# Turning a pair's first block of gathered rows one step earlier in an expert loop on Trainium2

## What is computed

```python
cap = int(math.ceil(CAP_FACTOR * K * N / E))          # 2 * 16384 / 8 = 4096 rows for each expert
disp = jnp.zeros((E, cap, D), x.dtype).at[e_flat, p_flat].add(x_rep * kmask[:, None])
h = jax.nn.gelu(jnp.einsum('ecd,edh->ech', disp, w1) + b1[:, None, :], approximate=False)
y = jnp.einsum('ech,ehd->ecd', h, w2) + b2[:, None, :]
yk = y[e_flat, p_flat]
w = gvals.reshape(-1).astype(x.dtype)
out = (yk * w[:, None]).reshape(N, K, D).sum(axis=1)
```

## Time and profile before

| | us |
|---|---|
| median of 3 runs | 5787.27 |
| lowest and highest | 5783.33, 5816.49 |
| the profiled execution's own time | 5797.3 |
| its span, from the first instruction to the last | 5795.6 |
| TensorE busy in it | 5178.6 (89%) |
| VectorE busy | 2885.5 (50%) |
| mean granted TensorE clock | 0.924 |

### The profile page before, as it was taken

One profiled execution on the slowest core, in us unless ns is written; L12 is line 12 of the kernel. 1 busy time (PEld: TensorE's weight loads), 2 busy tenths in 40 slices (PEclk: granted clock), 3 DMA queues, 4 the chain that ended last, 5 costly groups with the idle time before them and its releaser, 6 DMA issues. The chain is left out here.

```text
span 5795.6 us, 218499 instructions
## 1 busy us (share of the span) xinstructions
PE 5178.6 (89%) x98967; PEld 3339.4 (58%) x98967; DVE 2885.5 (50%) x6705; ACT 1707.7 (29%) x2823; POOL 941.6 (16%) x940
## 2 busy tenths in 40 slices
PE   5999999999999999999999857899999999999990
PEld 3556565665656556566565644566665666666660
DVE  6667676777767667676776639211111111111116
ACT  3433333343333334333333310111121121112113
POOL 0000000000000000000000000344444445445440
PEclk9899998999999999999999868999999999999995
DMA  1000000000000000000000000222222222222227
GB/s 31 22 19 26 26 23 29 19 29 23 22 30 19 29 23 22 30 19 29 23 22 29 15 31 4 62 32 49 53 32 49 38 47 49 38 47 34 38 31 236
DMA packets 211402, 207.31 MB, mean 36 GB/s; under 512 B 57314, under 2 KB 199715, under 8 KB 210467
## 3 DMA queue, kind: packets, MB, share of 16 engines
q0 software_dynamic: 57984, 69.29, 7.6%
q1 hardware_dynamic: 135970, 108.67, 6.1%
q10 hardware_dynamic: 16640, 16.78, 0.9%
HBM read 107.08 MB, written 85.49 MB: 33 GB/s over the span
## 5 line engine op out<-in xcount | busy, mean ns | idle before, releaser
L1473 PE MATMUL bank<-gathered_T,w1s 128*128 128x512 f32 x2048 | 951.5, 625 | 88.1 <-DVE gathered_T L1411 88.1
L1484 PE MATMUL bank<-w2s,hidden_T 128*128 128x256 f32 x4096 | 894.6, 379 | 0.0
L1484 PEld LDWEIGHTS bank<-w2s,hidden_T 128*128 128x128 f32 x4096 | 775.8, 190 | 117.7 <-issue 15.3
L1443 ACT ACTIVATE hidden_T<-bank,b_expert 128x512 f32<-128x512 f32 x512 | 351.8, 687 | 1588.7 <-PE bank L1473 1588.7
L1473 PEld LDWEIGHTS bank<-gathered_T,w1s 128*128 128x128 f32 x2048 | 408.5, 201 | 593.4 <-issue 591.8
L1418 DVE TENSOR_TENSOR result_rows<-bank,b2s 128x512 f32<-128x512 f32 x128 | 88.6, 692 | 1169.3 <-PE bank L1484 1169.3
L1150 POOL MEMSET tri<- 128x128 f32 x1 | 0.2, 210 | 3436.3 <-POOLq L337 3436.3
L1369 POOL DMA_INDIRECT sum_rows<-result_rows,block_index_out x256 | 403.0, 1574 | 110.5 <-issue 60.1
L901 PE MATMUL bank<-np,p20W 128*128 128x512 f32 x768 | 379.1, 624 | 7.9 <-issue 5.3
L901 PE MATMUL bank<-xT_and_z_out,ctrlW 128*128 128x512 f32 x768 | 381.6, 620 | 3.5 <-issue 3.5
L1411 DVE COPY gathered_T<-bank 128x512 f32<-128x512 f32 x128 | 88.4, 691 | 555.0 <-PE bank L1462 541.1
(11 more groups left out here) (289 smaller groups left out, 7609.3 us busy)
## 6 DMA issues: line engine op xcount, KB each, us to landing
x<-L_attn_hidden SPq DMA_DIRECT2D x33, 512.0 KB, 3.8
out_squares<-L_attn_hidden SPq DMA_DIRECT2D x32, 512.0 KB, 3.6
x_rows<-x SPq DMA_DIRECT2D x32, 512.0 KB, 3.2
sum_rows<-x SPq DMA_DIRECT2D x32, 512.0 KB, 4.2
sums<-sum_rows SPq DMA_DIRECT2D x16, 1024.0 KB, 6.8
out<-sums ACTq DMA_DIRECT2D x16, 1024.0 KB, 5.8
w1s<-L_ffn_w SPq DMA_DIRECT2D x8, 1024.0 KB, 5.0
w2s<-L_ffn_w SPq DMA_DIRECT2D x8, 1024.0 KB, 7.6
```

The costliest lines, as they stand in the source:

```text
L1443: nc.scalar.activation(hT[:, j, m, :], ring["h", j, m][:, :], ACT.Gelu, bias=b1e[:, par, m:m + 1]).then_inc(hT_ready, 1)
L1473: ins = nc.tensor.matmul(ps[:, :], w1s[:, par, k, m * P:(m + 1) * P], xgT[:, j, k, :], start=k == 0, stop=k == 1)
L1484: ins = nc.tensor.matmul(ps[:, i * D:(i + 1) * D], hT[:, j, m, s0:s0 + P], w2s[:, par, m, :], start=m == 0, stop=m == MT - 1)
```

## The change

The turn of block 0 moves. Before, it stands at the beginning of its own pair. Now the turn of the next pair's block 0 stands in this pair between h 1 and y 1. The very first one stands ahead of the loop, into banks 0 and 1 by name and with a semaphore of its own, `first_turned`. In `order` the entries `("xT", 0, k)` move behind those of h 1, so that all entries in between use a bank that is two further back. VectorE copies block 1's turned rows in its part for j = 0 and the next pair's block 0 in its part for j = 1, ahead of the y of the same j; `xg_used` moves with them. The last pair's additional turn works on rows that GpSimd gathers anyway and that no product uses.

```diff
--- before.py
+++ after.py
@@ -1306,13 +1306,15 @@
         biased, iout_ready, y_free = sem("y_biased"), sem("iout_ready"), sem("y_free")
         y_stored = [sem(f"y_stored{i}") for i in range(2)]
         filled, b1_ready, b1_cur, passed = sem("filled"), sem("b1_ready"), sem("b1_cur"), sem("wait_passed2")
+        first_turned = sem("first_block_turned")
         freed = {w: sem(f"freed_by_{w}") for w in ("act", "dve")}
         order = []
-        order += [(("xT", 0, k), "dve") for k in range(2)]
+
         order += [(("h", 0, m), "act") for m in range(MT)]
         order += [(("xT", 1, k), "dve") for k in range(2)]
         order += [(("y", 0, t), "dve") for t in range(SPB // 2)]
         order += [(("h", 1, m), "act") for m in range(MT)]
+        order += [(("xT", 0, k), "dve") for k in range(2)]
         order += [(("y", 1, t), "dve") for t in range(SPB // 2)]
         ring = Bank(order, banks, filled, freed)
 
@@ -1404,14 +1406,13 @@
 
                 def body(e, par, pair, n, j):
                     dve.wait_ge(w_loaded[par], e * 24 + (48 - par * 24))
-                    if j == 0:
-                        for q in range(2):
-                            for k in range(2):
-                                dve.wait_ge(filled, ring.full(pair, ("xT", q, k)))
-                                V.tensor_copy(xgT[:, q, k, :], ring["xT", q, k][:, :]).then_inc(xgT_ready, 1)
-                                dve.wait_ge(xgT_ready, pair * 4 + 2 * q + k + 1)
-                                dve.sem_inc(ring.freed["dve"], 1)
-                            dve.sem_inc(xg_used, 1)
+                    q = 1 - j
+                    for k in range(2):
+                        dve.wait_ge(filled, ring.full(pair, ("xT", q, k)))
+                        V.tensor_copy(xgT[:, q, k, :], ring["xT", q, k][:, :]).then_inc(xgT_ready, 1)
+                        dve.wait_ge(xgT_ready, pair * 4 + 2 * j + k + 3)
+                        dve.sem_inc(ring.freed["dve"], 1)
+                    dve.sem_inc(xg_used, 1)
                     dve.wait_ge(y_free, pair + 2)
                     for t in range(SPB // 2):
                         dve.wait_ge(filled, ring.full(pair, ("y", j, t)))
@@ -1424,6 +1425,11 @@
                     for i in range(SPB):
                         ins = V.tensor_scalar(ysb[:, j, i, :], ysb[:, j, i, :], wr[:, j, i, bass.ds(e, 1)], None, ALU.mult)
                     ins.then_inc(y_ready, 1)
+                for k in range(2):
+                    dve.wait_ge(first_turned, k + 1)
+                    V.tensor_copy(xgT[:, 0, k, :], banks[k][:, :]).then_inc(xgT_ready, 1)
+                dve.wait_ge(xgT_ready, 2)
+                dve.sem_inc(xg_used, 1)
                 loop(dve, body)
 
             @block.scalar
@@ -1453,27 +1459,29 @@
                 nc.tensor.transpose(banks[7][:, 0:E * MT], b1r[:, :], ident[0:E * MT, 0:E * MT]).then_inc(b1_ready, 1)
                 pe.wait_ge(b1_ready, 2)
 
-                def turn(pair, j):
-
+                def rows_turned(ps, j, k):
+                    for i in range(SPB):
+                        ins = nc.tensor.transpose(ps[:, i * P:(i + 1) * P], xg[:, j, i, k * P:(k + 1) * P], ident[:, :])
+                    return ins
+
+                def turn(pair, j, now):
                     pe.wait_ge(gathered[j], pair * (16 * SPB) + 16 * SPB)
                     for k in range(2):
-                        ps = ring.take(pe, pair, ("xT", j, k))
-                        for i in range(SPB):
-                            ins = nc.tensor.transpose(ps[:, i * P:(i + 1) * P], xg[:, j, i, k * P:(k + 1) * P], ident[:, :])
-                        ins.then_inc(filled, 1)
+                        rows_turned(ring.take(pe, now, ("xT", j, k)), j, k).then_inc(filled, 1)
+
+                pe.wait_ge(gathered[0], 16 * SPB)
+                for k in range(2):
+                    rows_turned(banks[k], 0, k).then_inc(first_turned, 1)
 
                 def body(e, par, pair, n, j):
                     pe.wait_ge(w_loaded[par], e * 24 + (48 - par * 24))
-                    if j == 0:
-                        turn(pair, 0)
                     pe.wait_ge(xgT_ready, n * 2 + 2)
                     for m in range(MT):
                         ps = ring.take(pe, pair, ("h", j, m))
                         for k in range(2):
                             ins = nc.tensor.matmul(ps[:, :], w1s[:, par, k, m * P:(m + 1) * P], xgT[:, j, k, :], start=k == 0, stop=k == 1)
                         ins.then_inc(filled, 1)
-                    if j == 0:
-                        turn(pair, 1)
+                    turn(pair + j, 1 - j, pair)
                     for t in range(SPB // 2):
                         ps = ring.take(pe, pair, ("y", j, t))
                         for i in range(2):
```

## The result

The changed kernel takes 5638.6 us (median of 4 runs, 5619.9 to 5641.9), the kernel before, with one more run beside it, 5792.1 us (4 runs). The ratio is 0.9732, with a 95% interval from 0.9707 to 0.9758: 2.7% faster. The profiled execution took 5641.9 us, with a span of 5640.1.

A forecast was written before the change was run, and what follows sets the result against it. TensorE was taken to bound the expert stage, waiting once a pair for VectorE's copies of turned rows, then running slow. Savings 92.2 + 59.9 - 0.9 = 151.2 us; 5787.3 - 151.2 = 5636 us, range 5622 to 5664.

The forecast's parts named there:

- The wait: At each pair's beginning, TensorE's idle time for VectorE's copies of turned rows goes, tails included: 92.2 us saved.
- The clock: First-layer products of block 0, slowed behind turn and wait, return to full clock: 59.9 us over 31 pairs.
- rival 1: Block 0's first-layer products stay slow for another reason; only 91.3 us saved, 5696 us; chance 0.06.
- The turn: Block 0's transposes cost the same in their new place; one added turn behind the last pair costs 0.9 us.
- The pauses that stay: Seven TensorE waits at experts' ends, now before block 0's first-layer products: no clock loss taken, 13.5 us at most.
- The rows that are asked for earlier: Next block 0's gathered rows land by 34 us at the latest, wanted at 42.2: eight to 13 us left.
- Rival 3: Next rows come late, TensorE stands before the last second-layer group; at 20 us lateness 5856 or 5916 us; chance 0.01.
- The loop's return: TensorE's return to the loop's start, formerly under the same idle time, costs nothing that shows.
- Rival 2: A pause or fetch at the loop's return shows: small 5648 us, chance 0.05; large 5754 us, chance 0.02.
- Rival 4: TensorE's clock is not kept over long stretches without pause; at 15 us a pair 5869 us; chance 0.02.

The follow-up runs named there:

- the version without the drain: Changed kernel without TensorE's wait at each expert's end for its own products; SyncE waits for the filled banks instead: 5607.9 us, run again 5636.8 us.

## Why the prediction was right

**The time.** 5636 was forecast, 5638.6 measured, 151.2 us of saving against 153.5 by the medians and 150.1 in the experts' stretch. The runs bear the mechanism out term by term, as follows. That the time itself was met within 3 us is partly luck: the median of the kernel before, from which the saving is taken, lay between 5781 and 5792 us in the comparisons of this document.

**The wait (92.2 us).** The idle time fell from 88.1 to 7.0 us where 7 were forecast, one wait of 0.9 and the experts' pauses of 6.1. From start to start, with the tails and the added turn in it, everything but h fell by 91.5 us, where 92.2 - 0.9 = 91.3 were forecast. The run with additional products, which has the wait without the slow clock, gives the same: its stretch is 91.1 us longer than the changed kernel's. Three things apart from the wait lie in that difference: the first h 0 is 2.8 us shorter there (13.73 against 16.51), the h 0 of 24 pairs 0.11 us longer (13.84 against 13.73), 2.6 us, and seven h 0 0.1 us shorter, 0.7, since no pause stands right in front of them. That makes 92.0; 0.6 of it is time that the additional products themselves cost against the kernel before. The remaining 91.4 leave nothing over for the new order of banks.

**The clock (59.9 us).** Busy time of the first layer fell by 58.7 us; with products in the idle time the stretch fell by 59.0, of which 57 belong to the 31 pairs. This was the term that was taken from a reading rather than from a wait, and rival 1 doubted it. Rival 1 falls with two runs: h 0 is fast behind a filled wait in its old place, and slow behind an idle one in the new place. The 1.2 us missing from 59.9 are the first pair, whose h 0 took 16.51 us against 15.72 before, and the seven h 0 behind the pauses at 0.1 us each.

**The turn (0.88 us each).** Five turns in place of one gave 0.87 us for each.

**The pauses that stay (0 of up to 13.5 us).** h behind the seven pauses lasts 13.83 or 13.84 us, so 0.1 us each; 31 pauses of 1.1 us confirm it. The 6 us that the working gave as the bound of a further gain, if work queued ahead hid these pauses, were too few: without them the stretch is 7.9 to 8.3 us shorter, because each has a tail of 0.16 us and slows the h behind it by 0.1. It took an edit of its own to get that.

**The rows that are asked for earlier.** The working said that block 0's gathers are issued by 26.6 us after the pair's start and wanted at 42.2. The timeline of GpSimd in the changed kernel, in the pair whose h 0 starts at 4233.94, has the last one:

```profile
4259.62 0.95 POOL L1359 DMA_INDIRECT gathered_rows<-x_rows,block_index  x1 [0.30 <-issue]
```

It is issued by 4260.57, 26.6 us after the start, as forecast, and the turn follows at 4276.09, at 42.2. When it lands, the working had 0.9 us too late: it added the 2.7 us to the end of the gather's row, but they count from its beginning. In the run with late gathers TensorE waits for the rows before 32 turns in the loop, and each time it goes on 2.7 to 3.0 us after the fourth gather's row begins. In the pair shown above it goes on at 4288.71, and the fourth gather is

```profile
4285.85 0.95 POOL L1359 DMA_INDIRECT gathered_rows<-x_rows,block_index  x1 [0.30 <-issue]
```

So the rows are in by about 4262.4, and the margin is 13.7 us against 12.9 forecast. In the late run the fourth gather begins 44.3 us after the pair's start instead of 25.7, 18.6 later; less the margin of 13.7 that is 4.9 us, the wait that it shows. Rival 3 was thus a true mechanism that this order of GpSimd's work does not set off: made real, it cost 7.7 us a pair and turned the gain into a loss. Its price was too low in one point. It let 4.9 us of waiting a pair merely use up the gain; with 5.0 us in the mean the stretch was 96 us longer than before, most of it from the slow clock behind the wait.

**The loop's return.** Rival 2 did not occur; the timeline has no gap behind y 1 within an expert. The queue that carries instructions moved 3 packets in 1814 us of the loop (2 before), and in the version without the drain TensorE is busy over the whole stretch, returns and all. The fetch that the Trainium skill gives to a taken branch out of the loaded pages (Runtime: NRT & Kernel Launch, Instruction fetch mechanics) is not in this trace either; whether these returns leave the loaded pages at all, no run shows.

**The clock under long load.** Rival 4 did not occur. The granted clock was 1.00 over 1813 us in which TensorE was busy for 1807, and in the version without the drain over 1804 us without a pause:

```profile
3682.00:5486.00 1804.00, 1804.00 (x6616) 1213.04 (x6615) 249.96 (x507) 371.11 (x530) 901.29 (x878) 1.00 0.25 45
```

## What to carry to other kernels

A short wait once in a loop can cost more than its length when TensorE stands idle in it: here 3 us of waiting cost 4.9, while pauses of 1.1 us cost little beyond themselves. Look for a group of products that is slower than its twin, and add that to the wait's price before deciding whether it is worth removing. The cure is to issue the small step that another engine must finish ahead of a long group that does not need it, and before doing so to count, from the same anchor, when its input arrives; that margin is what the move spends.

## What the runs showed of the hardware

- Idle times of 2.53 us lowered TensorE's granted clock in 29 of 31 pairs and left it alone in two. Between busy stretches, pauses of up to 1.21 us never lowered it (31 pairs, and seven pauses of 0.7 to 1.1). Idle times of 2.0 to 3.1 us behind a turn always did (31 pairs; in the seven with the short ones another 0.7 to 1.2 us stood ahead of the turn). The price was 1.5 to 1.8 us, in five pairs of before 3.1.
- The length of the last pause is not all that counts: the very first h 0, 0.9 us behind a turn with 10 us of idle time before it, took 15.7 to 16.5 us in all runs but the one with additional products, which ran in that place and left it at 13.7.
- Float32 transposes on TensorE kept the clock up, 40 of them in 4.37 us (granted clock 1.00 in them and behind them).
- TensorE held 2.4 GHz for 1813 us of float32 products on this one core, and for 1804 us without any pause in the version without the drain.
- A wait of TensorE for its own last product costs 0.8 us from start to start (y 1 takes 14.66 us in place of 13.81), with an outer loop's return 1.3 (15.11 us).
- A gather of 128 rows is in 2.7 to 3.0 us after its row on GpSimd begins, 1.8 to 2.0 after the row ends (the 32 waits of the run with late gathers).
